# Attention stage: one round of statistics for both norms, squares of x3 on ScalarE, later steps for the second norm

## The reference

```
x = x + _L1_conv_ref(_ln_c(x), ...)                       # x3 = x2 + attention of norm 1
t = t + _L1_ffn_ref(_ln_t(t), gate_w, gate_b, ...)        # norm 2 of x3, gate logits, softmax, top 8
def _ln_c(v, eps=1e-06): return (v - mean(v)) / sqrt(var(v) + eps)     # over the 64 channels; _ln_t with 1e-05
```

## Time and profile before

| | us |
|---|---|
| median of 3 runs | 1866.84 (1864.80 to 1868.62) |
| the profiled execution | 1866.96 |
| its span, first to last instruction | 1865.2 |
| TensorE matmul busy | 1439.8 (77%) |
| VectorE busy | 1384.8 (74%) |
| ScalarE busy | 1218.7 (65%) |
| GpSimd busy | 1398.2 (75%) |

### The profile page before, as it was taken

The page is one execution under the profiler, slowest core; times in us unless marked ns, Lnnn a source line. Parts: engine busy times, 40 slices in busy tenths (PEclk is TensorE's granted clock), DMA queues, the critical chain, the costliest instruction groups (busy, mean ns, idle before and its releaser), DMA issues. The chain is left out here.

```text
span 1865.2 us, 23730 instructions
## 1 busy us (share of the span) xinstructions
PE 1439.8 (77%) x5369; PEld 588.6 (32%) x5369; DVE 1384.8 (74%) x2395; ACT 1218.7 (65%) x2321; POOL 1398.2 (75%) x1029
## 2 busy tenths in 40 slices
PE   3888888888888883799981879999999999925200
PEld 1233333333333321366650523333333333204200
DVE  1888898989988992599974548999999999961000
ACT  2767777777777764599971468888898889620000
POOL 2988888888888890078879049999999999901476
PEclk8999999999999997899995889999999999965555
DMA  4588878888888765959995437888988888561011
GB/s 150 160 233 250 267 242 258 252 262 250 259 249 257 211 203 183 404 231 420 423 390 240 167 92 241 290 272 278 294 287 281 274 287 251 189 174 40 2 2 2
DMA packets 111403, 429.77 MB, mean 230 GB/s; under 512 B 44672, under 2 KB 47648, under 8 KB 66208
## 3 DMA queue, kind: packets, MB, share of 16 engines
q1 hardware_dynamic: 91376, 423.77, 69.5%
q10 hardware_dynamic: 16432, 4.29, 1.4%
q0 software_dynamic: 3456, 0.19, 0.2%
HBM read 257.89 MB, written 170.01 MB: 229 GB/s over the span
## 5 line engine op out<-in xcount | busy, mean ns | idle before, releaser
L599 DVE SCALAR_TENSOR_TENSOR pst<-xn,kk,pst 128x512 f32<-128x512 f32 x448 | 336.1, 750 | 8.2 <-PE pst L431 2.0
L431 PE MATMUL pst<-xn,taps 128*128 128x512 f32 x512 | 250.4, 612 | 89.6 <-DVE acc L599 89.6
L541 POOL TENSOR_TENSOR x_and_products<-tap_products,x_and_products 128x512 f32<-128x512 f32 x192 | 245.3, 1278 | 29.9 <-ACT tap_products L509 2.5
L1508 POOL TENSOR_SCALAR exp_q<-exp_q 128x512 f32<-128x512 f32 x128 | 189.7, 1482 | 73.1 <-ACT exp_q L1459 73.1
L925 DVE SCALAR_TENSOR_TENSOR pss<-region,bn,pss 128x256 f32<-128x256 f32 x432 | 195.7, 489 | 45.4 <-PE pss L837 44.9
L509 ACT ACTIVATE tap_products<-xn,kk 128x512 f32<-128x512 f32 x320 | 212.7, 709 | 13.6 <-POOL x_and_products L541 9.0
L548 POOL TENSOR_TENSOR x_ring<-acc,x_and_products 128x512 f32<-128x512 f32 x128 | 163.9, 1280 | 66.5 <-DVE acc L599 65.2
L1503 POOL TENSOR_TENSOR sq_norm<-x_ring 128x512 f32<-128x512 f32 x128 | 188.9, 1476 | 5.7 <-DVE x_ring L1555 2.3
L541 POOL TENSOR_TENSOR x_and_products<-tap_products,x_ring 128x512 f32<-128x512 f32 x128 | 163.5, 1278 | 19.8 <-ACT tap_products L509 19.8
L874 POOL TENSOR_TENSOR x_block<-x_block,region 128x2048 f32<-128x2048 f32 x28 | 155.6, 5558 | 20.2 <-DMA x_block<-x_scratch 16.7
L431 PEld LDWEIGHTS pst<-xn,taps 128*128 128x128 f32 x512 | 92.4, 191 | 234.8 <-issue 234.6
(11 more groups left out here) (237 smaller groups left out, 2867.9 us busy)
## 6 DMA issues: line engine op xcount, KB each, us to landing
rstd_wide<-rstd_scratch SPq DMA_DIRECT2D x128, 512.0 KB, 7.9
x_ring<-in_x SPq DMA_DIRECT2D x32, 1024.0 KB, 10.7
x_scratch<-x_ring SPq DMA_DIRECT2D x32, 1024.0 KB, 4.3
xl_scratch<-wx SPq DMA_DIRECT2D x32, 1024.0 KB, 8.7
region<-xl_scratch SPq DMA_DIRECT2D x32, 1024.0 KB, 12.6
x_ring<-x_scratch SPq DMA_DIRECT2D x32, 1024.0 KB, 5.2
rstd_of_channels<-rstd_scratch SPq DMA_DIRECT2D x64, 512.0 KB, 7.7
out<-x_ring SPq DMA_DIRECT2D x32, 1024.0 KB, 6.6
```

The costliest lines, as they stand in the source:

```text
L431: m = pe.matmul(wide(pst[g % 2]), taps[:, n * P:(n + 1) * P], tap_rows(g, t), start=(n == 0), stop=(n == len(mine) - 1))
L541: pool.tensor_tensor(xr[:, g % XR, :], prod[:, q % NP, :, :].rearrange("p r w -> p (r w)"), xr[:, g % XR, :] if n else x_tile(g), ALU.add) ...
L599: dve.scalar_tensor_tensor(out=out, in0=tap_rows(g, t), scalar=kk[:, t:t + 1], in1=wide(pst[g % 2]), op0=ALU.mult, op1=ALU.add).then_inc(a ...
L1508: pool.tensor_scalar(e, e, 1.0, None, ALU.min).then_inc(clipped, 1)
```

## The change

One round now holds the statistics of both norms: block k of the first norm and block k - 4 of the second. stat_of_norm, which the first stage of the kernel already fills, has for each norm weights that put its sums into its own 16 of 32 rows, so the matmuls of the second norm add into the same PSUM tile (start on the first norm, stop on the last). The chain of square, variance, Relu, Ln and Exp then runs once per round, with a column of epsilons per row. The squares of x3 go from GpSimd's loop to ScalarE's, behind square_x2(). The lags of the second norm's part move: STATS from 24 to 26, SQ3 from 20 to 21, GATE from 30 to 31, GSCALE from 30 to 32, BEST, BEST_AT and EXPSUM by two; LOAD goes from -1 to 1. The ring of squares of x3 has 8 places for 6.

```diff
-            SQSLOTS = (6, 6)
+            SQSLOTS = (6, 8)
...
-            LOAD, SQ2, QUERY, QSCALE, QMAP, DENOM, BYZ, ATTEND, X3, SQ3, TURN = -1, 6, 15, 16, 17, 18, 18, 20, 20, 20, 27
-            STATS = (10, 24)
+            LOAD, SQ2, QUERY, QSCALE, QMAP, DENOM, BYZ, ATTEND, X3, SQ3, TURN = 1, 6, 15, 16, 17, 18, 18, 20, 20, 21, 27
+            STATS = (10, 26)
+            BEHIND = (STATS[1] - STATS[0]) // TPB
+            ROUNDS = NBLK + BEHIND
             QCLIP = 16
-            GATE, GSCALE, BEST, BEST_AT, EXPSUM = 30, 30, 33, 35, 37
+            GATE, GSCALE, BEST, BEST_AT, EXPSUM = 31, 32, 35, 37, 39
...
+            def norms_in(n):
+                return [(l, n - BEHIND * l) for l in range(2) if 0 <= n - BEHIND * l < NBLK]
...
-                def rstd_to_dram(l, k):
-                    n = round_of[l, k]
+                def rstd_to_dram(n):
                     sp.wait_ge(rstd_ready, n + 1)
-                    for b in range(B):
-                        sp.dma_start((r3_d, r4_d)[l][k, b, :].rearrange("(j n) -> j n", n=TILE),
-                                     rstd[16 * b:P:32, n % 2, :]).then_inc(rstd_out[n % 2], 16)
+                    for l, k in norms_in(n):
+                        for b in range(B):
+                            sp.dma_start((r3_d, r4_d)[l][k, b, :].rearrange("(j n) -> j n", n=TILE),
+                                         rstd[16 * l + 8 * b:P:32, n % 2, :]).then_inc(rstd_out[n % 2], 16)
...
-                    for j in range(TPB):
-                        m = pe.matmul(psm[32 * j:32 * j + 32, :], stat32[:, :], x_tile(TPB * k + j), start=True, stop=True)
+                    for l, k in norms:
+                        for j in range(TPB):
+                            m = pe.matmul(psm[32 * j:32 * j + 32, :], stat_of[:, l, :], x_tile(TPB * k + j),
+                                          start=(l, k) == norms[0], stop=(l, k) == norms[-1])
                     m.then_inc(mean_ready, 1)
-                    pe.wait_ge(squared[l], TPB * (k + 1))
+                    for l, k in norms:
+                        pe.wait_ge(squared[l], TPB * (k + 1))
...
-                    for l in range(2):
-                        if (k := block_at(t, STATS[l])) is not None:
-                            stats_of(l, k)
+                    if (n := round_at(t)) is not None:
+                        stats_of(n)
...
+                def square_x3(g):
+                    act.wait_ge(x3_ready, g + 1)
+                    if g >= SQSLOTS[1]:
+                        act.wait_ge(second_ready, round_of(1, (g - SQSLOTS[1]) // TPB) + 1)
+                    act.activation(sq[1][:, g % SQSLOTS[1], :], x_tile(g), ACT.Square).then_inc(squared[1], 1)
...
                     if (g := tile_at(t, SQ2)) is not None:
                         square_x2(g)
+                    if (g := tile_at(t, SQ3)) is not None:
+                        square_x3(g)
...
-                def square_x3(g):
-                    pool.wait_ge(x3_ready, g + 1)
-                    if g >= SQSLOTS[1]:
-                        pool.wait_ge(second_ready, round_of[1, (g - SQSLOTS[1]) // TPB] + 1)
-                    pool.tensor_tensor(sq[1][:, g % SQSLOTS[1], :], x_tile(g), x_tile(g), ALU.mult).then_inc(squared[1], 1)
...
-                    if (g := tile_at(t, SQ3)) is not None:
-                        square_x3(g)
```

More of the change, by code:

```diff
@@ L1250, in build_program, with round_of, rstd_written, round_at @@
             blk = ph.enter_context(nc.Block())
-            LOAD, SQ2, QUERY, QSCALE, QMAP, DENOM, BYZ, ATTEND, X3, SQ3, TURN = -1, 6, 15, 16, 17, 18, 18, 20, 20, 20, 27
-            STATS = (10, 24)
+            LOAD, SQ2, QUERY, QSCALE, QMAP, DENOM, BYZ, ATTEND, X3, SQ3, TURN = 1, 6, 15, 16, 17, 18, 18, 20, 20, 21, 27
+            STATS = (10, 26)
+            BEHIND = (STATS[1] - STATS[0]) // TPB
+            ROUNDS = NBLK + BEHIND
             QCLIP = 16
-            GATE, GSCALE, BEST, BEST_AT, EXPSUM = 30, 30, 33, 35, 37
+            GATE, GSCALE, BEST, BEST_AT, EXPSUM = 31, 32, 35, 37, 39
             STEPS_D = NT + EXPSUM + 1
-            order = sorted((TPB * k + STATS[l], l, k) for l in range(2) for k in range(NBLK))
-            round_of = {(l, k): n for n, (_, l, k) in enumerate(order)}
+            def round_of(l, k):
+                return k + BEHIND * l
+            def norms_in(n):
+                return [(l, n - BEHIND * l) for l in range(2) if 0 <= n - BEHIND * l < NBLK]
+            def rstd_written(n):
+                return rstd_out[n % 2], sum(16 * B * len(norms_in(m)) for m in range(n % 2, n + 1, 2))
+            def round_at(t):
+                n, rest = divmod(t - STATS[0], TPB)
+                return n if rest == 0 and 0 <= n < ROUNDS else None
             def tile_at(t, lag):
@@ L1316, in rstd_to_experts @@
                 def rstd_to_experts(k):
-                    n = round_of[1, k]
-                    sp.wait_ge(rstd_out[n % 2], 32 * (n // 2 + 1))
+                    sp.wait_ge(*rstd_written(round_of(1, k)))
                     if k >= 2:
@@ L1343, in _ @@
                         load(k)
-                    for l in range(2):
-                        if (k := block_at(t, STATS[l] + 2)) is not None:
-                            rstd_to_dram(l, k)
+                    if (n := round_at(t - 2)) is not None:
+                        rstd_to_dram(n)
                     if (h := pair_at(t, TURN + 1)) is not None:
@@ L1359, in _, with stats_of @@
             def _(pe):
[L1360 to L1367, removed]
+                def stats_of(n):
+                    norms = norms_in(n)
+                    for l, k in norms:
+                        if l == 0:
+                            pe.wait_ge(*loaded_x2(k))
+                        else:
+                            pe.wait_ge(x3_ready, TPB * (k + 1))
                     if n:
                         pe.wait_ge(msq_done, n)
-                    for j in range(TPB):
-                        m = pe.matmul(psm[32 * j:32 * j + 32, :], stat32[:, :], x_tile(TPB * k + j), start=True, stop=True)
+                    for l, k in norms:
+                        for j in range(TPB):
+                            m = pe.matmul(psm[32 * j:32 * j + 32, :], stat_of[:, l, :], x_tile(TPB * k + j),
+                                          start=(l, k) == norms[0], stop=(l, k) == norms[-1])
                     m.then_inc(mean_ready, 1)
-                    pe.wait_ge(squared[l], TPB * (k + 1))
+                    for l, k in norms:
+                        pe.wait_ge(squared[l], TPB * (k + 1))
                     if n:
                         pe.wait_ge(clamped, n)
-                    for j in range(TPB):
-                        m = pe.matmul(pse[32 * j:32 * j + 32, :], stat32[:, :], sq[l][:, (TPB * k + j) % SQSLOTS[l], :],
-                                      start=True, stop=True)
+                    for l, k in norms:
+                        for j in range(TPB):
+                            m = pe.matmul(pse[32 * j:32 * j + 32, :], stat_of[:, l, :], sq[l][:, (TPB * k + j) % SQSLOTS[l], :],
+                                          start=(l, k) == norms[0], stop=(l, k) == norms[-1])
                     m.then_inc(second_ready, 1)
@@ L1479, in _ @@
                 for t in range(0, STEPS_D):
[L1480 to L1485, removed]
+                    if (n := round_at(t - 2)) is not None:
+                        rsqrt(n)
+                    if (n := round_at(t - 1)) is not None:
+                        square_mean(n)
                     if (k := block_at(t, EXPSUM)) is not None:
@@ L1526, in _, with variance @@
             def _(dve):
-                def variance(l, k):
-                    n = round_of[l, k]
+                def variance(n):
                     dve.wait_ge(second_ready, n + 1)
@@ L1586, in _ @@
                         scale_query(g)
-                    rounds = [(l, k) for l in range(2) if (k := block_at(t, STATS[l] + 1)) is not None]
                     if (g := tile_at(t, TURN)) is not None:
                         turn_x3(g)
-                    for l, k in rounds:
-                        variance(l, k)
+                    if (n := round_at(t - 1)) is not None:
+                        variance(n)
                     if (g := tile_at(t, X3)) is not None:
```

16 lines of the change are left out of this document (6 added, 10 removed).

## The result

The changed kernel takes 1976.38 us (median of 4 runs, 1971.14 to 1980.66) against 1866.24 (4 runs, 1864.80 to 1868.62): a ratio of 1.0588, 95% interval 1.0559 to 1.0617. Its profiled execution took 1974.97 us, with a span of 1973.2.

A forecast was written before the change was run, and what follows sets the result against it. TensorE, running back to back, was taken as the bound, GpSimd as second limit. New waits of 3.96 us per period over 28 periods (111) plus 3 for filling and draining: 1866.96 + 111 + 3 = 1981 us, range 1913 to 2000.

The forecast's parts named there:

- The layout: TensorE's starts and waits over one period of four tiles: 20.78 us against 16.82, 3.96 more.
- step 2: Steps are counted t mod 4; after the change all statistics stand in this one, and its attend() is time 0.
- into 3: Stretch with four groups of statistics, query and gate before the denominator: query 4.56, denominator 6.63, attend 7.60 us.
- into 0: Stretch with a query alone: denominator 10.48, attend 11.45 us, TensorE waiting about 1.2 us for q_map.
- into 1: Stretch with query and gate: gate 14.96, attend 16.93 us, the gate waiting about 1.7 us for scale_logits().
- into 2: Stretch with a query alone: denominator 19.81, attend 20.78 us, TensorE waiting about 1.2 us.
- q_map inside a clip: VectorE's q_map starting during GpSimd's clip, taken as 1.10 us long in steps 3 and 1, otherwise 0.74.
- Filling and draining: Later gates, logits and maxima at the stage's ends: +3 us, between -5 and +10.
- The parts costed at nothing: Squares moved to ScalarE, SP's later transfer of the first norm's factors and later block load: no cost expected.
- GpSimd as the real bound: Rival, 8%: GpSimd set the period, so relief makes the kernel faster, 1859 us or 1827.
- The rival of the denominators alone: Rival, 13%: only denominators wait, the gate of step 1 finds its logits scaled; 1934 or 1913 us.
- The locked q_map: Rival, 8%: q_map on VectorE is locked out for GpSimd's whole clip; period 22.8 us, 2037 us in all.

The follow-up runs named there:

- e7b_split: Changed kernel with gates and scaling at lag 32, channels' factors first on SP, sums of x two steps before sums of squares: 1869.11 us, ratio 1.0001.
- e3_squares_pool: Changed kernel with the squares of x3 back on GpSimd, ahead of its clip: 1981.73 us, ratio 1.0630.
- e2_gates_even: Changed kernel with gates and scaling both at lag 32, so gates in even steps again: 1923.98 us, ratio 1.0308.
- e4_before_half_clip: Kernel before the change, with GpSimd clipping only 256 of 512 columns of the exponential: 1863.18 us, ratio 0.9979.
- e1_scale_31: Changed kernel with scale_logits() one step earlier (GSCALE 31 for 32): 1954.87 us, ratio 1.0462.
- e5_denominator_19: Changed kernel with the denominator and all that follows it one step later, gates and scaling as changed: 1996.08 us, ratio 1.0682.

## Why the prediction was right

*The bound.* That GpSimd's 16.68 of 16.81 was not the limit held: half clips left the period at 16.81, and in e7b_split GpSimd has 10.91 us to do and the period is the same.

*The layout.* From attend() of step 2 at 0, forecast and measured (1409.73 as 0): query into 3 at 4.56 and 4.52, denominator 6.63 and 6.59, attend 7.60 and 7.55; into 0, denominator 10.48 and 10.34; into 1, gate 14.96 and 14.67, attend 16.93 and 16.64; into 2, denominator 19.81 and 19.44, attend 20.78 and 20.40. Every wait of this period is where it was put and ends on what was named. Three terms were somewhat too long:
- q_map inside a clip was taken at 1.10 us from a row at the start of the stage; it measured 1.01, in steps 3 and 1, and 0.73 in step 0, where it starts ahead of the clip as forecast (in step 2, where nothing waits for it, 0.82, inside a clip too). Steps 3 and 1 make 0.18 of the 0.38 us by which the period was too long.
- From x3 of step 3 to x3 of step 0, MAX8 between, 4.16 were taken, and it measured 3.95 (1418.34 to 1422.29); 0.09 of that is the q_map of step 3.
- From the gate to the attend of step 2, 5.82 were laid out, and it measured 5.73: the q_map of step 1.

*The sum.* 3.96 us per period over 28 periods made 111; measured, 20.40 less 16.82 is 3.58, or 100 us. Filling and draining were taken at 3, between -5 and 10; what is left of the span's 108.0 is 8 us. The two errors have opposite signs, and the total came out at 108 for 114: closer, by luck, than its terms.

*The parts costed at nothing.* Squares: shown (e3_squares_pool). The single variance, and the later lags of the second norm: e7b_split has them all and the time of before. The factors for the channels go out 19.0 us after the attend() of step 2 (1428.71), 18.5 in the layout. Their transfer takes 9.6 us to land (median) where it took 7.7, which is still early enough:

```profile
L1327 SPq DMA_DIRECT2D rstd_of_channels<-rstd_scratch x64: 483/586/1003, 1084.8 to 1693.9; - x64
...
who waited for it (us, times):
  DVE query L1550: 5.8, 1
DMA to landing us min/median/max: 4.6/9.6/12.4
```

One wait of 5.8 us at the stage's start, as before (5.9), and two more of 0.89 and 0.26 us without a named releaser; the second is in the one period that took 20.76 us. e2_gates_even showed how little cover this had.

*The rivals.* GpSimd as the real bound fell with e4_before_half_clip. The rival of the denominators alone fell with the 1.41 us of the gate; but e1_scale_31, in which the gate does not wait, came to 1955 us and not to 1934 or 1913: that rival had left out that an earlier scaling delays VectorE's other work. The locked q_map fell too: that of step 3 ends at 1420.02 and the clip beside it at 1420.34 (1418.86 + 1.48), and a q_map locked out would have ended behind it. It is longer inside a clip than alone, 1.01 or 0.82 against 0.73 us. The Trainium skill's rule in "SBUF — State Buffer", section "Who interferes with whom", that the later of the two blocks until the first is through, does not describe this pair; the trace agrees with it for q_z alone.

## What to carry to other kernels

In a pipeline written out by hand, what lies between a producer's input and its consumer on the in-order engine is cover: before merging or moving work, write out for every step what TensorE does between attend() and the next denominator(), and compare it with the length of the chain (2.5 us here). Merging two rounds into one and moving the gates by a step took next to nothing away from TensorE, left two of four steps bare, and cost 6%. With the gates back in even steps, the factors sent first and the statistics split over two steps, the same merged round cost nothing; with gate and statistics side by side, the first norm's sums of x early and a later denominator the kernel gained 0.8%. When a wait is taken away, look at whose turn moved on the engine that served it, and on SP's queue what stands ahead of a transfer that is needed soon.

## What the runs showed of the hardware that was not expected

The granted clock can fall inside an otherwise busy stage behind two short waits. In e5_denominator_19 TensorE was busy for 10.20 us at 1.00, waited 1.20, ran one query, waited 1.41, and was then granted 0.50, the level of 1.2 GHz, for the next 5.45 us. The change itself has waits of 0.91, 1.41 and 0.92 us, spread over 20.40, and its period kept 1.00. In e2_gates_even it fell behind one longer wait. Windows view of that run, around the query that waited:

```profile
1452.64:1455.90 3.26, 1.02 (x3) 0.22 (x2) 0.93 (x3) 1.86 (x5) 0.53 (x1) 1.00 0.45 172
1455.90:1457.81 1.91, 1.10 (x2) 0.27 (x3) 1.91 (x4) 1.91 (x4) 1.21 (x1) 0.78 0.33 131
1457.81:1461.38 3.57, 3.57 (x4) 1.51 (x5) 1.76 (x3) 1.72 (x4) 1.58 (x3) 0.50 1.08 371
```

The wait itself cost 2.24 us. Behind it, at 0.50, it is 3.57 us from a denominator to the next query (1457.81 to 1461.38), where the same three starts two steps earlier are 1.72 apart (1448.00 to 1449.72). What decides between the two outcomes is open: in e5_denominator_19 the clock kept 1.00 in 6 of the 18 periods. Waits of 1.01 us for the query and 1.41 or 1.42 for the gate went by without a fall in five of them (1450.42 and 1452.93 are one case) and were followed by one in five others; waits of 1.50 and 1.41 (1238.20 and 1240.71) left it at 1.00. The Trainium skill, "TensorE: Matmul & The Clock Gate", section "The HAM clock gate", says that the clock follows how busy TensorE has lately been; the falls here, each behind waits, agree.
